# LayerNorm statistics inside a recurrent block: transposes on TensorE against partial sums sent through DRAM

## The chip, the cores and the metric

The kernel runs on one core of one Trainium2 chip. The metric is the device time of one execution in microseconds (us), lower is better. TensorE (PE) multiplies matrices and transposes through an identity matrix, VectorE (DVE), ScalarE (ACT) and GpSimd (POOL) work elementwise, and the SyncE queue (SP) issues nearly all transfers. The engines run their own instruction streams in order and wait for each other by semaphores.

## What is computed

```python
# attention-like block: a recurrence over 32 chunks of 16 positions, for each (batch, head)
def step(W, kv):
    kc, vc = kv
    z = einsum('bhsd,bhde->bhse', kc, W)
    grad = einsum('bhsd,bhse->bhde', kc, (z - vc) * inv_n)
    return (W - LR * grad, z)
out = zs ...                                   # (B, S, 512)
mu = mean(out, axis=-1); var = var(out, axis=-1)
out = (out - mu) * rsqrt(var + 1e-5) * ln_gamma + ln_beta
x = layernorm(x + out @ Wo.T)                  # then a mixture of 8 experts, top 2, and a shared expert
```

The change concerns `mu` and `var` of the recurrence's output: one mean and one variance for each of 2048 tokens, over 512 features.

## The kernel before, in words

The 2048 tokens are ordered so that one step of the recurrence gives 64 tokens and two steps give one **tile** of 128 tokens. There are 16 tiles, 0 to 15. The program is written out slot by slot: each of the 32 steps is two slots, the even one with `scan_z` (z by 64 small matmuls, L548) and `scan_r` (the residual, DVE L559, then four masks on ACT, L562), the odd one with `scan_g` (64 small matmuls, L573, then the new W copied out of PSUM by ACT, L580). The order of every engine's work is that in which `slot` calls the helpers; no planner is involved.

After the scan's own instructions, each slot adds work of three kinds:

- the pipeline of the tiles, by the list `STAGES`: an entry (d, pe, fn) runs fn(i) in slot 4i + d, entries that are not for PE first. For tile i, `out_rows` (POOL, L602 and L604) writes z into `zst` in slot 4i+3; `zt` (DVE, L613) transposes it by blocks of 32x32 into `zT` in slot 4i+4; `t_one` (PE, L618) transposes zT by four 128x128 blocks into bank 6 in slot 4i+5, so that a row of the bank is one token; `hi_z` (ACT, L623) and, in slot 4i+6, `stats_one` (DVE, L628, L589, L590) split zT in two parts for exact products and take the statistics from bank 6; `t_wo_` (PE, L649) multiplies by Wo in slot 4i+7; `stats_two` (DVE L654, L589, L590, POOL L591, L592, L658) scales by the first rstd, adds x and takes the second statistics in slot 4i+8; `norm_two` (ACT, L661) normalizes in slot 4i+9 and stores; `t_three` (PE, L672) transposes the result in slot 4i+10, `router` (L684) follows. So `stats_two(i-1)` stands in the same slot as `zt(i)`, behind it, and `t_three(i-1)` in the slot of `stats_one(i)`.
- filler for PE: the projections of the next quarter (`products`, L444, with the rotary arrangement on DVE L474, L479, L485, L490 and POOL L471, L475), and from slot 47 on the shared expert (`gate_up_steps` L755 with DVE L731 and L255, `down_steps` L779 with DVE L782), whose weights are split on ACT and DVE (L240, L243) and on ACT and POOL (L230, L231).
- loads, all on SP, in program order: `fetch_x`, the stores of `norm_two` and `t_three`, and at slot 48 `load_d(0)` and `load_g(1)`, at slot 64 `load(3)`.

The scan ends with slot 63; slots 64 to 71 drain the tiles. Then come the routing, the rest of the shared expert and the expert stage.

`DV.op`, `PO.op` and the like append an instruction and return a token (semaphore, value); a token given as an argument is waited for. `SP.dma` does the same for a transfer.

Of the kernel before, what the change touches and what calls it, by code (L numbers as in the profile page):

```python
# [6 lines left out]
F32 = mybir.dt.float32  # L7
F32R = mybir.dt.float32r
ALU = mybir.AluOpType
# [5 lines left out]
EPS = 1e-5  # L15
# [80 lines left out]
def program(nc, xT, xtok, wkT, wvT, woT, gam, bet, wg, wgu, wd, wsgu, wsd, cosd, sind, maskd, negid, identd, lowd, constd, upd, out):  # L96
    ctx = ExitStack()
    with ctx:
        def sem(name):
            return ctx.enter_context(nc.semaphore(name))  # L100

        def sb(stack, name, shape, dt=F32):
            return stack.enter_context(nc.sbuf_tensor(name, [128] + shape, dt))

        PE, DV, AC, PO, SP = (Queue(sem(n)) for n in ("s_pe", "s_dve", "s_act", "s_pool", "s_sp"))
        bank = [ctx.enter_context(nc.psum_tensor(f"bank{i}", [128, 512], F32)) for i in range(8)]


        ident = sb(ctx, "ident", [128])
# [3 lines left out]
        mhalf = sb(ctx, "mhalf", [1])  # L113
        mv = sb(ctx, "mv", [4, 2])
        rstd = sb(ctx, "rstd", [4, 2])
# [143 lines left out]
        pa = ExitStack()  # L259
        size = {"late": 0, "first": 0}  # L260

        def part(stack, key, name, shape, dt=F32):
            size[key] += int(np.prod(shape))
            return sb(stack, name, shape, dt)
# [4 lines left out]
        r = part(pa, "late", "r", [2, 2, 512])  # L269
# [3 lines left out]
        zst = part(pa, "late", "zst", [4, 2, 2, 32])  # L273
        zT = part(pa, "late", "zT", [512])
        colsum = part(pa, "late", "colsum", [512])
        oh = part(pa, "late", "oh", [4, 128], F32R)
# [4 lines left out]
        onesr = part(pa, "late", "onesr", [128], F32R)  # L281
        mask = part(pa, "late", "mask", [64])
        wgs = part(pa, "late", "wgs", [4, 8])
        part(pa, "late", "padl", [288])

        vst0 = sb(pa, "vst0", [8, 256])
        vst = (vst0, vst1)
# [48 lines left out]
        d_wkk = [Stream(sem(f"d_wk{k}")) for k in range(4)]  # L336
        d_wvk = [Stream(sem(f"d_wv{k}")) for k in range(4)]
        d_g0 = Stream(sem("d_g0"))
        d_xt = [Stream(sem("d_xt0")), Stream(sem("d_xt1"))]


# [28 lines left out]
        t_mh = PO.op(lambda e: e.memset(mhalf[:], -0.5))  # L370
# [65 lines left out]
        free = {i: () for i in range(8)}  # L436
# [92 lines left out]
        for h in (0, 1):  # L529
            t = PE.op(lambda e, h=h: e.matmul(bank[2 + h][:, 0:256], ident[:], negi[:], start=True, stop=False, skip_group_check=True),  # L530
                      t_ident, t_c2, *free[2 + h])
# [52 lines left out]
        state = {}  # L584
        mvfree = {}

        def norm_stats(src, tok, slot):

            a = DV.op(lambda e: e.bn_stats(st[:, slot, :], src), tok, mvfree.get(slot))  # L589
            b = DV.op(lambda e: e.bn_aggr(mv[:, slot, :], st[:, slot, :]), a)  # L590
            c = PO.op(lambda e: e.tensor_scalar(rstd[:, slot, 0:1], mv[:, slot, 1:2], EPS, None, ALU.add), b)  # L591
            return PO.op(lambda e: e.tensor_tensor(rstd[:, slot, 1:2], rstd[:, slot, 0:1], mhalf[:], ALU.pow), c, t_mh)  # L592

        def out_rows(i):

            par = (i // 4) % 2
            rd = (rdone[2 * i, 0], rdone[2 * i, 1], rdone[2 * i + 1, 0], rdone[2 * i + 1, 1])
            for m in range(2):
                rr = r[:, i % 2, m, :].rearrange("p (a b e) -> p a b e", a=8, b=2)
                zz = za[:, m, :].rearrange("p (a e) -> p a e", a=8)  # L600
                vv = vst[par][:, (2 * i + m) % 8, :].rearrange("p (a e) -> p a e", a=8)
                a = PO.op(lambda e, rr=rr, zz=zz: e.tensor_tensor(zz, rr[:, :, 0, :], rr[:, :, 1, :], ALU.add), *rd)  # L602
                zo = zst[:, :, m, :, :]
                b = PO.op(lambda e, zz=zz, vv=vv, zo=zo: e.tensor_tensor(  # L604
                    zo, zz.rearrange("p (g b) e -> p g b e", g=4), vv.rearrange("p (g b) e -> p g b e", g=4), ALU.add),
                    a, state.get("zT"))
            zst_done[i] = b
            if i % 4 == 3:
                scan_done[i // 4] = (b, gdone[2 * i + 1, 0], gdone[2 * i + 1, 1])
            state["zst"] = b  # L610

        def zt(i):
            state["zT"] = DV.op(lambda e: e.transpose(zT[:], zst[:].rearrange("p a b c d -> p (a b c d)")), state["zst"], state.get("T1"), state.get("oh"))  # L613

        def t_one(i):
            b = 6
            for g in range(4):
                t = PE.op(lambda e, g=g: e.transpose(bank[b][:, g * 128:g * 128 + 128], zT[:, g * 128:g * 128 + 128], ident[:]),  # L618
                          state["zT"], *free[b], inc=(g == 3))
            state["T1"] = t  # L620

        def hi_z(i):
            state["oh"] = AC.op(lambda e: e.activation(oh[:].rearrange("p a b -> p (a b)"), zT[:], ACT.Copy), state["zT"], state.get("WO"))  # L623
# [1 line left out]
        def stats_one(i):  # L625


            state["ol"] = DV.op(lambda e: e.tensor_tensor(ol[:].rearrange("p a b -> p (a b)"), zT[:], oh[:].rearrange("p a b -> p (a b)").bitcast(F32), ALU.subtract),  # L628
                                state["oh"], state["zT"], state.get("WO"))
            state["n1"] = norm_stats(bank[6][:], state["T1"], 0)  # L630
            free[6] = ((DV.sem, DV.count),)

        def fetch_x(i):

# [159 lines left out]
        def down(w, q):  # L794
            for _ in down_steps(w, q):
# [3 lines left out]

        STAGES = [(3, False, fetch_x), (3, False, out_rows), (4, False, zt), (5, True, t_one), (5, False, hi_z), (6, False, residual),
                  (6, False, stats_one), (7, True, t_wo_), (8, False, stats_two),
                  (9, False, norm_two), (10, True, t_three), (11, True, router)]
        later = []
# [13 lines left out]
        def slot(n):  # L819
            q, loc = n // 16, n % 16  # L820
            if n == 48:
                early[:] = [(Q.sem, Q.count) for Q in (PE, DV, AC, PO)]
            todo = [(pe, fn, (n - d) // 4) for d, pe, fn in STAGES
                    if (n - d) % 4 == 0 and 0 <= (n - d) // 4 < NT]
# [102 lines left out]

        LAST = 4 * NT - 4 + STAGES[-1][0]

# [524 lines left out]
```

How the kernel before makes its waits and increments, by code:

```python
    def play(self, eng):  # L69
        for it in self.items:
            if it[0] == "w":
                eng.wait_ge(it[1], it[2])
            elif it[0] == "c":
                _, used, at, fns, other, sem, by = it
                with eng.If_cmp(used[id(self)], at, "IS_GT"):
                    for fn in fns:
                        ins = fn(eng)
                    ins.then_inc(sem, by)
                with eng.Else():
                    other(eng).then_inc(sem, by)
            elif it[0] == "r":
                it[1][id(self)] = eng.to_reg(eng.value_load(it[2], min_val=0, max_val=RT - FULL))
            else:
                ins = it[1](eng)
                if it[2] is not None:
                    ins.then_inc(it[2], it[3])
```

## Time and profile before

| what | value |
|---|---|
| median of three runs | 717.73 us (717.64 to 718.1) |
| profiled execution, its own time | 717.65 us |
| its span, first to last instruction | 715.8 us |
| granted TensorE clock, mean | 0.994 |
| PE busy | 695.0 us (97%) |
| DVE busy | 461.5 us (64%) |
| ACT busy | 341.5 us (48%) |
| POOL busy | 330.0 us (46%) |

The profile is one execution. A view by line groups the instructions of one source line; a timeline puts them in order of start, merging equal neighbours, with the idle time before them and what ended it in brackets. The chain of waits goes back from the last instruction to whatever released each step. Most waits of PE in it are short, since PE has filler in nearly every slot.

### The profile page before, as it was taken

The page shows a single profiled execution, that of the slowest core. Times are in us where ns is not written, and L with a number is a line of the kernel's source. Part 1 is how long each engine was busy: PE and PEld are TensorE (multiplying, and loading weights), DVE is VectorE, ACT ScalarE, POOL GpSimd, SP SyncE. Part 2 cuts the span into 40 slices and gives each one's busy share as a digit, 9 for nine tenths or more (in the row PEclk, how much of TensorE's full clock was granted, in tenths as well). Part 3 has the DMA queues.
Part 4 walks back from the last instruction along what each step waited for, and adds up shares of the span by engine and source line. Part 5 has one row for each costly group of instructions (what it writes and reads, how often), then busy time and mean ns, then how long its engine had stood idle before and what let it go on. Part 6 is the DMA issues. An engine that isn't in the chain of part 4 may idle for free.

```text
span 715.8 us, 17650 instructions
## 1 busy us (share of the span) xinstructions
PE 695.0 (97%) x7388; PEld 583.7 (82%) x7388; DVE 461.5 (64%) x767; ACT 341.5 (48%) x662; POOL 330.0 (46%) x350
## 2 busy tenths in 40 slices
PE   9999999999999999999999999999999899999994
PEld 7767888788877777887888999999988878888883
DVE  4996564585755555378876676666576637767555
ACT  5654444454555442341123677767777542141232
POOL 3667556677555433011003665566574326526232
PEclk9999999999999999999999999999999999999998
DMA  8121131121242414000063798999788966414212
GB/s 291 66 75 47 47 104 47 62 89 34 105 135 76 150 47 147 29 14 1 0 235 103 239 326 291 311 319 327 253 274 259 317 189 196 119 68 118 74 73 89
DMA packets 59584, 102.86 MB, mean 144 GB/s; under 512 B 5296, under 2 KB 20400, under 8 KB 59504
## 3 DMA queue, kind: packets, MB, share of 16 engines
q1 hardware_dynamic: 53824, 83.11, 34.2%
q0 software_dynamic: 5680, 18.62, 8.5%
q8 instruction: 59, 0.97, 0.6%
q14 instruction: 21, 0.17, 0.1%
HBM read 79.95 MB, written 21.76 MB: 142 GB/s over the span
## 4 chain that ended last, share of the span: by engine, by line
PE 79%; DVE 10%; ACT 6%; issue 3%; POOL 0%; POOLq 0%; DVEq 0%; ACTq 0%
PE bank L755 20%; PE bank L444 12%; PE bank L779 10%; PE bank L1203 10%; PE bank L649 7%; PE bank L1250 5%; PE bank L573 4%; PE bank L548 4%; PE bank L1219 2%; PE bank L1176 2%; PE bank L684 2%; DVE GL L255 2%; ACT GH L254 2%; DVE sg L731 1%; ACT ah L254 1%
## 5 line engine op out<-in xcount | busy, mean ns | idle before, releaser
L231 POOL TENSOR_TENSOR xl<-RAW,xh 128x1024 fp32r<-128x1024 f32 x31 | 74.9, 2417 | 113.1 <-ACT xh L230 79.9
L254 ACT ACTIVATE ah<-sg 128x512 fp32r<-128x512 f32 (+1 forms) x64 | 33.6, 525 | 157.9 <-DVE sg L731 157.9
L755 PE MATMUL bank<-XH,GH 128*128 128x512 f32 x256 | 101.8, 398 | 1.5 <-ACT GH L254 0.9
L755 PE MATMUL bank<-XH,GL 128*128 128x512 f32 x256 | 99.9, 390 | 0.0
L755 PE MATMUL bank<-XL,GH 128*128 128x512 f32 x256 | 99.7, 389 | 0.0
L255 DVE TENSOR_TENSOR GL<-RAW,GH 128x1024 fp32r<-128x1024 f32 (+2 forms) x63 | 80.6, 1317 | 9.7 <-ACT GH L254 8.3
L591 POOL TENSOR_SCALAR rstd<-mv 128x1 f32<-128x1 f32 x48 | 15.3, 318 | 135.8 <-DVE mv L590 135.1
L1133 POOL DMA_INDIRECT xg<-x1d,idxu x39 | 49.9, 1281 | 57.0 <-DVE idxu L1114 41.2
L1203 PE MATMUL bank<-RH,GH 128*128 128x256 f32 x256 | 73.8, 288 | 0.8 <-ACT RAW L1260 0.4
L1203 PE MATMUL bank<-RH,GL 128*128 128x256 f32 x256 | 72.4, 283 | 0.0
L1203 PE MATMUL bank<-RL,GH 128*128 128x256 f32 x256 | 72.4, 283 | 0.0
L559 DVE TENSOR_TENSOR r<-bank,vst 128x256 f32<-128x256 f32 x64 | 26.5, 423 | 66.9 <-PE bank L548 66.2
L731 DVE TENSOR_TENSOR sg<-sg,bank 128x512 f32<-128x512 f32 (+1 forms) x64 | 35.0, 548 | 50.6 <-PE bank L755 32.4
L254 ACT ACTIVATE GH<-RAW 128x1024 fp32r<-128x1024 f32 (+2 forms) x67 | 63.5, 998 | 1.4 <-DMA RAW<-in_wgu 1.0
L255 DVE TENSOR_TENSOR al<-sg,ah 128x512 fp32r<-128x512 f32 (+1 forms) x64 | 37.8, 591 | 37.8 <-ACT ah L254 37.8
L562 ACT ACTIVATE r<-r,mask 128x128 f32<-128x128 f32 x128 | 41.0, 391 | 41.5 <-DVE r L559 41.4
L755 PEld LDWEIGHTS bank<-XH,GH 128*128 128x128 f32 x256 | 48.1, 188 | 12.1 <-ACT XH L704 1.3
L755 PEld LDWEIGHTS bank<-XH,GL 128*128 128x128 f32 x256 | 48.0, 188 | 10.4
L755 PEld LDWEIGHTS bank<-XL,GH 128*128 128x128 f32 x256 | 48.1, 188 | 9.4
L444 PE MATMUL bank<-xh,GH 128*128 128x512 f32 x128 | 53.9, 421 | 0.0
L779 PE MATMUL bank<-xh,ah 128*128 128x512 f32 x128 | 50.8, 397 | 1.3 <-DVE x L782 1.0
L1308 POOL DMA_INDIRECT xg<-yd,SI x32 | 34.1, 1064 | 37.7 <-DVE x L1316 23.3
(226 smaller groups left out, 1742.5 us busy)
## 6 DMA issues: line engine op xcount, KB each, us to landing
RAW<-in_wgu SPq DMA_DIRECT2D x21, 1024.0 KB, 8.6
RAW<-in_wd SPq DMA_DIRECT2D x21, 512.0 KB, 6.4
yd<-RAW SPq DMA_DIRECT2D x39, 256.0 KB, 7.5
RAW<-in_wsgu SPq DMA_DIRECT2D x14, 512.0 KB, 4.9
x<-in_xtok SPq DMA_DIRECT2D x16, 256.0 KB, 3.4
x1d<-x SPq DMA_DIRECT2D x16, 256.0 KB, 2.0
RAW<-in_wsd SPq DMA_DIRECT2D x8, 512.0 KB, 4.2
out_x<-x SPq DMA_DIRECT2D x16, 256.0 KB, 2.0
```

The lines of the kernel that those rows point to most:

```text
L231: b = PO.op(lambda e: e.tensor_tensor(DL[:, p, :, :], draw[:, rawp(w), :, :], DH[:, p, :, :].bitcast(F32), ALU.subtract), a, dloaded[w], *f)
L254: a = AC.op(lambda e: e.activation(hi, src, ACT.Copy), *tokens, *free)
L255: b = rest.op(lambda e: e.tensor_tensor(lo, src, hi.bitcast(F32), ALU.subtract), a, *tokens, *free)
L444: t = PE.op(lambda e, k=k, wt=wt, xx=xx, n=n: e.matmul(bank[b][:], wt[:, j, k, hg * 128:hg * 128 + 128], xx[:, k, :], start=(k == 0 and n ...
L562: rtok[h] = AC.op(lambda e, b=b: e.activation(r4[:, :, b, :], r4[:, :, b, :], ACT.Copy, scale=mask[:, 32 * b:32 * b + 1]), s, t_c2)
L649: t = PE.op(lambda e, k=k, aa=aa, ww=ww, n=n: e.matmul(bank[b][:], aa[:, k, :], ww[:, k, :], start=(n == 1), stop=(n == 12)), state["oh"], ...
L731: m = DV.op(lambda e: e.tensor_tensor(sg[:, w, 0:cols], sg[:, w, 0:cols], bank[bu][:, 0:cols], ALU.mult), a, tu)
L755: t = PE.op(lambda e, b=b, k=k, c=c, wt=wt, xx=xx, n=n: e.matmul(bank[b][:], wt[:, p, k, c:c + 128], xx[h][:, k, :], start=(n == 1), stop= ...
L779: t = PE.op(lambda e, b=b, k=k, j=j, aa=aa, ww=ww, n=n: e.matmul(bank[b][:], aa[:, ap, k, j * 128:j * 128 + 128], ww[:, p, k, :], start=(n ...
L1133: PO.items.append(("i", lambda e, h=h: e.indirect_dma_start(xg[:, j % 2, h, :], None, x1d, bass.IndirectOffsetOnAxis(ap=idxu[:, first + h: ...
L1203: t = PE.op(lambda e, b=b, k=k, c=c, wt=wt, xx=xx, n=n: e.matmul(bank[b][:, 0:256], wt[:, pw, k, c:c + 128], xx[:, p, k, :], start=(n == 1 ...
L1250: fns.append(lambda e, b=b, k=k, h=h, aa=aa, ww=ww, n=len(fns): e.matmul(bank[b][:], aa[:, p, k, h * 128:h * 128 + 128], ww[:, pw, k, :], ...
```

## The change

Before, the statistics are read from bank 6, which TensorE fills with four transposes for each tile. After, `t_one` is gone. A new `stat_z` in slot 4i+4, directly behind `zt` and ahead of `stats_two(i-1)`, takes statistics of four pieces of `zst` on DVE (each 128 partitions x 128 elements), which are partial: a token's 512 features lie in four groups of 32 partitions. The four results (24 numbers in each partition) go to a DRAM tensor by one transfer of 12 KB; SP waits until it has landed, and four further transfers bring them back into `sta`, such that a partition holds the four partial statistics of one token. `stats_one` then aggregates these in one instruction. The wait of `zt` for the transposes goes, and `zst` is freed by the last partial statistics. `hi_z`, `stats_one` and all else keep their slots.

```diff
+        stz = part(pa, "late", "stz", [4, 6])
+        sta = part(pa, "late", "sta", [4, 6])
+        d_stz, d_sta = Stream(sem("d_stz")), Stream(sem("d_sta"))
+        zsd = nc.dram_tensor("zsd", (128, 4, 6), F32, kind="Internal").ap()
@@ out_rows
-                    a, state.get("zT"))
+                    a, state.get("zread"))
@@
         def zt(i):
-            state["zT"] = DV.op(lambda e: e.transpose(zT[:], ...), state["zst"], state.get("T1"), state.get("oh"))
-
-        def t_one(i):
-            b = 6
-            for g in range(4):
-                t = PE.op(lambda e, g=g: e.transpose(bank[b][:, g * 128:g * 128 + 128], zT[:, g * 128:g * 128 + 128], ident[:]),
-                          state["zT"], *free[b], inc=(g == 3))
-            state["T1"] = t
+            state["zT"] = DV.op(lambda e: e.transpose(zT[:], ...), state["zst"], state.get("oh"))
+
+        def stat_z(i):
+            for m in range(4):
+                t = DV.op(lambda e, m=m: e.bn_stats(stz[:, m, :], zst[:, :, m // 2, m % 2, :]), state["zst"], state.get("stz"))
+            state["zread"] = t
+            w = SP.dma(zsd, stz[:], d_stz, t, state.get("sta"))
+            state["stz"] = w
+            view = zsd.rearrange("(g r) m s -> m r g s", g=4)
+            for m in range(4):
+                state["sta"] = SP.dma(sta[32 * m:32 * m + 32, :, :], view[m], d_sta, w, state.get("n1a"))
@@ stats_one
-            state["n1"] = norm_stats(bank[6][:], state["T1"], 0)
-            free[6] = ((DV.sem, DV.count),)
+            b = DV.op(lambda e: e.bn_aggr(mv[:, 0, :], sta[:]), state["sta"])
+            state["n1a"] = b
+            c = PO.op(lambda e: e.tensor_scalar(rstd[:, 0, 0:1], mv[:, 0, 1:2], EPS, None, ALU.add), b)
+            state["n1"] = PO.op(lambda e: e.tensor_tensor(rstd[:, 0, 1:2], rstd[:, 0, 0:1], mhalf[:], ALU.pow), c, t_mh)
@@
-        STAGES = [(3, False, fetch_x), (3, False, out_rows), (4, False, zt), (5, True, t_one), (5, False, hi_z), (6, False, residual),
+        STAGES = [(3, False, fetch_x), (3, False, out_rows), (4, False, zt), (4, False, stat_z), (5, False, hi_z), (6, False, residual),
```

## Rows read from the trace of the kernel before

**Rows 1.** The page, part 4: the chain that ended last, shares by engine.
```profile
PE 79%; DVE 10%; ACT 6%; issue 3%; POOL 0%; POOLq 0%; DVEq 0%; ACTq 0%
```

**Rows 2.** View of source line L618: duration ns min/median/max, first and last start.
```profile
L618 PE MATMUL bank<-ident,zT x64: 272/273/329, 47.5 to 278.2; 128*128 128x128 f32 x64
```

**Rows 3.** Timeline of tile 6: start us, us, engine, line, count, [idle before <- releaser].
```profile
134.07 0.87 DVE L559 TENSOR_TENSOR r<-bank,vst 128x256 f32<-128x256 f32 x2 [3.32 <-PE bank L548]
...
134.86 0.70 DVE L613 STREAM_TRANSPOSE zT<-zst 128x512 f32<-128x512 f32 x1
...
138.21 0.27 POOL L658 TENSOR_SCALAR mv<-mv,rstd 128x1 f32<-128x1 f32 x1
138.35 0.66 PE L618 MATMUL bank<-ident,zT 128*128 128x128 f32 x4
...
138.77 0.48 PE L444 MATMUL bank<-xh,GH 128*128 128x512 f32 x1
...
139.29 0.81 ACT L661 ACTIVATE x<-x,mv,rstd 128x512 f32<-128x512 f32 x1
...
141.36 0.66 PE L672 MATMUL bank<-ident,x 128*128 128x128 f32 x4
...
142.67 0.69 DVE L589 BATCH_NORM_STATS2 st<-bank 128x6 f32<-128x512 f32 x1
```

**Rows 4.** Lines of DVE by form: count, busy us, mean ns of one, idle before.
```profile
L589 DVE BATCH_NORM_STATS2 st<-bank 128x6 f32<-128x512 f32 x16 | 11.0, 689 | 0.0
...
L999 DVE TENSOR_TENSOR c<-c 128x128 f32<-128x128 f32 x1 | 0.3, 285 | 0.0
```

**Rows 5.** Chain of waits, routing stretch: start us, us, piece (small DVE operations in a row).
```profile
326.23 0.21 DVE c L999
...
326.46 0.23 DVE sel L1000
```

**Rows 6.** The page, part 6: DMA issues, KB each, median us from issue to landing.
```profile
x<-in_xtok SPq DMA_DIRECT2D x16, 256.0 KB, 3.4
x1d<-x SPq DMA_DIRECT2D x16, 256.0 KB, 2.0
```

**Rows 7.** Timeline of tile 3.
```profile
94.66 0.81 ACT L661 ACTIVATE x<-x,mv,rstd 128x512 f32<-128x512 f32 x1 [0.87 <-POOL mv L658]
...
95.76 0.66 PE L672 MATMUL bank<-ident,x 128*128 128x128 f32 x4
```

**Rows 8.** Timeline of tile 10.
```profile
194.44 0.71 DVE L613 STREAM_TRANSPOSE zT<-zst 128x512 f32<-128x512 f32 x1
...
198.10 0.81 ACT L661 ACTIVATE x<-x,mv,rstd 128x512 f32<-128x512 f32 x1 [0.66 <-POOL mv L658]
...
200.49 0.69 DVE L589 BATCH_NORM_STATS2 st<-bank 128x6 f32<-128x512 f32 x1
```

**Rows 9.** Timeline of tile 11, with the loads of slots 48 and 50.
```profile
206.45 0.38 SPq L62 DMA_DIRECT2D RAW<-in_wsd  x1
...
209.16 0.70 DVE L613 STREAM_TRANSPOSE zT<-zst 128x512 f32<-128x512 f32 x1
...
218.11 1.23 PE L573 MATMUL bank<-r,RAW 32*32 32x64 f32 x64 [0.41 <-ACT r L562]
...
219.02 1.05 ACT L230 ACTIVATE xh<-RAW 128x1024 fp32r<-128x1024 f32 x1
```

**Rows 10.** Timeline of tile 12, at its first filler behind the weights' split.
```profile
233.53 0.50 PE L755 MATMUL bank<-XH,GH 128*128 128x512 f32 x1 [0.33 <-DVE GL L243]
```

**Rows 11.** Timeline of tile 14, where banks 4 and 5 are evacuated.
```profile
263.27 1.27 DVE L782 TENSOR_TENSOR x<-bank,x 128x512 f32<-128x512 f32 x2
...
263.99 0.50 PE L779 MATMUL bank<-xh,ah 128*128 128x512 f32 x1
```

**Rows 12.** Timeline of tile 15, same place in the drain.
```profile
280.88 0.50 PE L779 MATMUL bank<-xh,ah 128*128 128x512 f32 x1 [0.99 <-DVE x L782]
```

**Rows 13.** Timeline of tile 0, its product with Wo.
```profile
54.89 0.47 PE L649 MATMUL bank<-OH,oh 128*128 128x512 f32 x1 [0.35 <-DVE OL L430]
```

More of the change, by code:

```diff
@@ L283, in program @@
         wgs = part(pa, "late", "wgs", [4, 8])
-        part(pa, "late", "padl", [288])
+        stz = part(pa, "late", "stz", [4, 6])
+        sta = part(pa, "late", "sta", [4, 6])
+        part(pa, "late", "padl", [240])
         vst0 = sb(pa, "vst0", [8, 256])
@@ L612, in zt @@
         def zt(i):
-            state["zT"] = DV.op(lambda e: e.transpose(zT[:], zst[:].rearrange("p a b c d -> p (a b c d)")), state["zst"], state.get("T1"), state.get("oh"))
-        def t_one(i):
-            b = 6
-            for g in range(4):
-                t = PE.op(lambda e, g=g: e.transpose(bank[b][:, g * 128:g * 128 + 128], zT[:, g * 128:g * 128 + 128], ident[:]),
-                          state["zT"], *free[b], inc=(g == 3))
-            state["T1"] = t
+            state["zT"] = DV.op(lambda e: e.transpose(zT[:], zst[:].rearrange("p a b c d -> p (a b c d)")), state["zst"], state.get("oh"))
+        def stat_z(i):
[7 more added lines that the diff above has]
+                state["sta"] = SP.dma(sta[32 * m:32 * m + 32, :, :], view[m], d_sta, w, state.get("n1a"))
         def hi_z(i):
```

## Prediction, made before the changed kernel was run

> **What bounds the kernel now.** I read first the chain that ended last [rows 1]: TensorE carries 79% of it, DVE 10%. Then the source line of the removed transposes [rows 2], to see that all 64 exist and stop with the scan's drain, and then timelines, one for each kind of tile. What the reader is to see in the timeline of tile 6 [rows 3] is an engine order with PE at full work: the transposes start at 138.35, the next projection at 138.77, and nobody waits in between. DVE has long pauses in the same stretch (3.32 us before the residual at 134.07). So PE time that is taken away here is worth its full length, as long as the other engines keep their present distance. The other timelines show where they don't have that distance: places at which PE waits, or all but waits, for something behind `stats_two` on DVE.
>
> **What goes.** Four transposes take PE 0.42 us in tile 6 (138.35 to 138.77) [rows 3]; one alone lasts 273 ns, pipelined [rows 2]. Sixteen tiles: 16 x 0.42 = 6.7 us, the most that the change can give. The bank-6 statistics also go from DVE, 689 ns for each tile [rows 4]; they stand behind `ol` and in front of DVE's pauses, where in most tiles nobody waits for DVE, so I count nothing for them.
>
> **What comes on DVE.** Four partial statistics of 128 elements each. The trace has none of that size. Nearest rows: the statistics of 512 elements last 689 ns, other DVE operations with 128 elements in and out 285 ns [rows 4], and such small operations follow each other in steps of 0.23 us [rows 5]. From below: four quarters of 0.69, thus 0.7 us; from above 4 x 0.285 = 1.14 us. I take 4 x 0.23 = 0.92 us, the row of operations in series. The Trainium skill has a rule against just this ("VectorE: DVE Perf Modes", section on the TRN2 errata): latency of SBUF-sourced operations is paid for each instruction, so one large tile pays it once and many small ones each time. Its table (58 cycles plus the elements, at 0.96 GHz) would make 4 x 0.19 = 0.78 us, its measured formula (elements plus 151 cycles) 4 x 0.29 = 1.16 us; the row of 285 ns agrees with the latter. No term below uses these figures.
>
> What matters is where the 0.92 us is put: directly behind `zt(i)` and in front of `stats_two(i-1)` in the same slot. Behind that runs a chain of short operations: DVE L654, L589, L590, POOL L591, L592, L658, ACT L661, and for that PE waits with L672. It all starts 0.92 us later.
>
> **Tiles with cover.** In tile 6, L658 ends at 138.21 + 0.27 = 138.48, L661 starts at 139.29 and ends at 140.10, L672 starts at 141.36 [rows 3]. After: L658 ends at 139.40, L661 at about 140.3, L672 is wanted at 141.36 - 0.42 = 140.94. Cover left 0.6 us, so the gain is whole: -0.42. By the same reading of their timelines this holds for eight tiles (1, 2, 4, 5, 6, 8, 9, 13): 8 x -0.42 = -3.4 us.
>
> **Tiles without.** In tile 3, L661 already waits 0.87 us for POOL, and ends at 94.66 + 0.81 = 95.47, L672 starts at 95.76 [rows 7]: 0.29 us of cover. After, L661 ends at 96.39 and L672 can't start before about 96.45, where the transposes' removal would have had it at 95.34. Against before: +0.7. Tile 7 has the same picture. Tile 10: L661 waits 0.66 us, starts at 198.10 [rows 8] and would end at 199.83, PE wants it about half a us before: +0.5. Tile 11: PE waits 0.41 us there for the masks on ACT, which stand behind L661 and the shared expert's steps [rows 9]; the gain is eaten: 0.
>
> From tile 12 on DVE also splits weights and evacuates banks 4 and 5, behind `stats_two` in the same slots. Tile 12: PE waits 0.33 us for DVE L243 [rows 10], which stands behind the new operations. The transposes' removal only makes this wait longer, and L243 comes 0.92 later: +0.9. Tile 14: L779 starts at 263.99, when the first of the two evacuations from 263.27 is done (1.27 us for two) [rows 11]: +0.9. Tile 15: L779 already waits 0.99 us for L782 [rows 12]: +0.9. In tile 0 the product with Wo waits 0.35 us for DVE L430 [rows 13]; the removed 0.69 stands against the added 0.92 and a wait for the transfers: +0.3.
>
> **Sum.** -3.4 + 0.7 + 0.7 + 0.5 + 0 + 0.9 + 0.9 + 0.9 + 0.3 = +1.5 us. After the drain the work is the same as before and moves as a whole.
>
> **What comes as transfers and waits.** DVE now waits in `stats_one(i)` for four transfers. From the start of `zT` the chain is: 0.70 transpose + 0.92 partial statistics + 2.0 us write (as the 256 KB store of x1, 2.0 us from issue to landing [rows 6]) + three more issues of 0.38 us on SP [rows 9] = 1.14 + 2.0 for the last read = 6.8 us, about 7.0 with the gaps. Room: in tile 6 from 134.86 to 142.67 are 7.8 us [rows 3], less the 0.42 that is gone: 7.4. In tile 10 from 194.44 to 200.49 are 6.05 us [rows 8]: there DVE waits about 1 us. The shorter tiles are 0, 3, 7, 10 and 14. Queued behind the waiting `bn_aggr` on DVE are the rotary operations L479, L485, L490, in tile 10 the split of x for the shared expert, and then the next residual; before that DVE has a pause of 3.3 us (that at 134.07 [rows 3]), so a wait of 1 us costs nothing, save the share in tile 0. POOL waits for the same result ahead of `out_rows(i+1)` and has more than 1 us as well. Bounds of a landing: 2.0 below (no transfer in this trace lands sooner), 3.4 above, the reads of x [rows 6]. With 3.4 for both the chain is 9.6 us, the wait 2.2 us in tiles like 6 (hidden, under 3.3) and 3.5 us in those like 10, which costs PE 1 to 2 us in each of four or five: up to +8 us.
>
> SP waits twice in each tile: for DVE, then about 2 us for the landed write. Behind it stand the stores of x1, the next `fetch_x` and, in tile 11, `load_d(0)` and `load_g(1)`. The latter were issued from 206.45, ahead of zT(11) at 209.16 [rows 9]; now they come behind its reads, at about 209.16 + 0.7 + 0.9 + 2.0 + 4 x 0.38 = 214.3. ACT wants load_d(0) at 219.02 [rows 9]: 4.7 us for a transfer of 512 KB. That is just enough, and ACT has filler work of PE behind it, so 0; were it 3 us later, the next W would be. The stores and `fetch_x` have a tile's length (15 us) to spare. `load(3)` in slot 64 moves equally, and is needed some tens of us later.
>
> So the forecast is 717.65 + 1.5 = 719.15 for the profiled execution, or by the median (717.73) 719.2 us.
>
> **Rivals.**
> (a) *DVE's extra time is covered everywhere*: the chain through POOL and ACT would have to catch up by the start of L672, and L243 and L782 by that of their matmuls. For it: DVE is 64% busy, and the 0.69 us that it loses comes back two slots later. Against it: five places where PE waits, or has under 0.3 us, in the trace of before. It gives 717.65 - 6.7 = 711.0. If only the three to four tiles on ACT's chain are covered, it gives -8 x 0.42 - 4 x 0.42 + 2.7 + 0.3 = -2.0, thus 715.7. Together 0.28.
> (b) *The round trip through DRAM becomes the bound* (the slower side): five dependent transfers of pieces of 96 and 24 bytes. The point from which it decides is a chain of 7.4 + about 2 us, where DVE's pause and POOL's distance to the next zst end. At 3.4 us a landing it costs up to 8 us (727 with the forecast's own loss), at 4.5 us each 16 x about 2 us = 30 us. For it: no transfer of such small pieces stands alone in the trace of before. Against it: 12 KB is nothing beside 256 KB that land in 2.0. The Trainium skill ("DMA: Bandwidth & Descriptors", table of specifications) speaks for it: below 512 bytes a descriptor makes the engine read, modify and write. It gives no time for this, and no row of before shows one. Chance 0.14.
> (c) *SP's order becomes the bound*: load_d(0) or load_g(1) come too late by the 8 us that they are moved, and ACT stands with W behind it. It decides from a landing of over 5 us plus its cover of 4 us; costs 1 to 3 us, once: 721. Chance 0.05.
> (d) *The transposes were no cost to PE*, since PE would only wait elsewhere: forecast without its gain, +4.9 or 722.5. Chance 0.05.
>
> The forecast has 0.48. A measurement of this kernel can tell about 0.2%, 1.4 us, from no change; the forecast's +1.5 lies on that line, so I split its share: 0.26 slower, 0.18 the same, 0.04 faster. Adding the rivals: slower 0.26 + 0.14 + 0.05 + 0.05 = 0.50, the same 0.18 + 0.04 of (a) = 0.22, faster 0.04 + 0.24 = 0.28. The range leaves out the full gain of (a) and the worst of (b): 713 to 725. The likeliest case's own range, from the bounds of the partial statistics (0.7 to 1.14 us in seven places: -1.5 to +1.5), is 717.7 to 720.7.
>
> **What would show it.** Right: no L618; the four partial statistics in steps near 0.23 us and 0.9 in sum; L661 ends about a microsecond later behind zT than before in every tile; PE waits for L661 at L672 in tiles 3, 7 and 10 and not in 6; longer waits of PE for L243 (tile 12) and L782 (tiles 14, 15); reads landed about 7 us after the start of zT, and DVE idle before `bn_aggr` for 1 us or less. Wrong: steps well under 0.2 us, or L661's chain caught up by POOL's pauses; or landings of 3 us and more with DVE idle over 3 us before `bn_aggr`; or ACT L230 waiting for its weights.

## The result, and the profile after

The changed kernel takes 722.55 us (median of five runs, 720.73 to 724.07); the kernel before, run beside it, 718.1 us (five runs, 717.64 to 719.46). The ratio is 1.0073, with a 95% interval of 1.0054 to 1.0093: slower by 4.4 us, where 1.5 was forecast. The measured time lies in the forecast's range of 713 to 725, but above what it gave as the likeliest case's own range, 717.7 to 720.7. The profiled execution took 723.94 us, with a span of 722.1.

The page of after, head and parts 1 and 4 (the chain that ended last), as [rows 1]:

```profile
span 722.1 us, 17659 instructions
...
PE 692.1 (96%) x7324; PEld 579.7 (80%) x7324; DVE 472.7 (65%) x815; ACT 340.5 (47%) x662; POOL 335.2 (46%) x350
...
PE 70%; DVE 14%; ACT 7%; issue 3%; POOL 3%; DMA 2%; SPq 1%; POOLq 0%; DVEq 0%; ACTq 0%
```

PE has 64 instructions fewer and is still on the chain, but with 70% of it instead of 79%: DVE, POOL and the transfers now stand in between. What PE waits for, of after (us in total, times, longest):

```profile
PE bank L789 <- DVE x L792: 3.7, 2, 2.2
...
PE bank L682 <- ACT x L671: 2.9, 4, 0.9
PE bank L659 <- DVE OL L434: 2.4, 1, 2.4
...
PE bank L765 <- DVE GL L243: 1.1, 2, 0.8
```

and the same view of before, where these were short or absent (L672, which is L682 of after, isn't in it):

```profile
PE bank L779 <- DVE x L782: 1.0, 1, 1.0
...
PE bank L649 <- DVE OL L430: 0.4, 1, 0.4
PE bank L755 <- DVE GL L243: 0.3, 1, 0.3
```

These four together are 10.1 us after and 1.7 before: 8.4 us of new waits against 6.7 us of transposes removed. That makes only +1.7. Most of the rest of the loss is time in which PE works, but at a lower clock; it comes below.

**A covered tile.** Timeline of tile 6 of after, to be laid beside [rows 3]:

```profile
137.56 0.70 DVE L617 STREAM_TRANSPOSE zT<-zst 128x512 f32<-128x512 f32 x1
...
138.18 0.83 DVE L622 BATCH_NORM_STATS2 stz<-zst 128x6 f32<-128x128 f32 x4
...
141.68 0.27 POOL L668 TENSOR_SCALAR mv<-mv,rstd 128x1 f32<-128x1 f32 x1
...
143.66 0.66 PE L682 MATMUL bank<-ident,x 128*128 128x128 f32 x4
...
144.88 0.25 DVE L638 BATCH_NORM_AGGREGATE mv<-sta 128x2 f32<-128x24 f32 x1
```

From the transpose to L668 it is 4.12 us where it was 3.35, so the chain of `stats_two` is later by 0.8, and PE doesn't wait.

**A tile without cover.** Timeline of tile 3 of after, as [rows 7]:

```profile
98.36 0.81 ACT L671 ACTIVATE x<-x,mv,rstd 128x512 f32<-128x512 f32 x1 [1.64 <-POOL mv L668]
...
99.22 0.66 PE L682 MATMUL bank<-ident,x 128*128 128x128 f32 x4 [0.87 <-ACT x L671]
```

ACT's wait went from 0.87 to 1.64 us, and PE, which did not wait, waits 0.87.

**By tile.** From one start of the product with Wo to the next tile's (for tile 0 from the start of zT(0)), after less before, read from the two timelines:

| tiles | forecast, each | measured |
|---|---|---|
| 2, 4, 5, 6, 8, 9, 13 | -0.42 | -0.40, -0.41, -0.40, -0.40, -0.34, -0.42, -0.40 |
| 1 | -0.42 | +1.12 |
| 3, 7 | +0.7 | +0.58, +0.59 |
| 10 | +0.5 | +0.54 |
| 11 | 0 | 0.00 |
| 12, 14 | +0.9 | +0.75, +0.81 |
| 15 | +0.9 | +2.37 |
| 0 | +0.3 | +1.64 |
| sum | +1.5 | +5.6 |

The stretch that holds all of this, from the start of zT(0) to the first gather of the expert stage, is the yardstick below. It takes 332.50 us before (45.80 to 378.30) and 338.14 after (46.36 to 384.50): +5.64. What lies outside it took 380.8 to 384.0 us in the ten profiled executions of this document, part of it by a fall of the clock that only five of them have there (last section). So differences of spans and of medians don't agree with the yardstick to the microsecond, and each of its numbers is that of one execution.

Three places stand out: tiles 0, 1 and 15. The timeline of tile 0 of after, to be laid beside [rows 13]:

```profile
53.79 0.26 DVE L638 BATCH_NORM_AGGREGATE mv<-sta 128x2 f32<-128x24 f32 x1 [1.28 <-DMA sta<-zsd]
...
54.60 2.35 DVE L434 TENSOR_TENSOR OL<-x,OH 128x512 fp32r<-128x512 f32 x2
...
54.99 1.41 POOL L479 TENSOR_TENSOR shuf<-shuf,sinT 128x512 f32<-128x512 f32 x1
...
57.09 0.47 PE L659 MATMUL bank<-OH,oh 128*128 128x512 f32 x1 [2.37 <-DVE OL L434]
...
57.40 0.40 PE L659 MATMUL bank<-OL,oh 128*128 128x512 f32 x1
...
59.19 0.63 PE L659 MATMUL bank<-OL,oh 128*128 128x512 f32 x1
```

The same two instructions of DVE in before, with POOL starting 0.2 us before they end:

```profile
53.45 1.29 DVE L430 TENSOR_TENSOR OL<-x,OH 128x512 fp32r<-128x512 f32 x2
...
54.54 1.34 POOL L475 TENSOR_TENSOR shuf<-shuf,sinT 128x512 f32<-128x512 f32 x1
```

PE stands still for 2.37 us, and then its matmuls last 0.63 instead of 0.40 us. And the drain of tile 15, as [rows 12]:

```profile
284.72 1.28 DVE L792 TENSOR_TENSOR x<-bank,x 128x512 f32<-128x512 f32 x2
285.46 0.50 PE L789 MATMUL bank<-xh,ah 128*128 128x512 f32 x1 [2.25 <-DVE x L792]
```

Behind both pauses the granted clock falls. PE by stretches of 1 us, after (stretch, PE busy (instructions), granted clock, DMA share, GB/s):

```profile
57.00:58.00 1.00, 0.91 (x4) 1.00 0.00 0
58.00:59.00 1.00, 1.00 (x5) 0.65 0.00 0
...
60.00:61.00 1.00, 1.00 (x4) 0.50 0.00 0
61.00:62.00 1.00, 1.00 (x34) 0.64 0.00 0
...
286.00:287.00 1.00, 1.00 (x6) 1.00 1.06 359
287.00:288.00 1.00, 1.00 (x6) 0.50 0.98 296
...
290.00:291.00 1.00, 1.00 (x5) 0.80 1.01 363
```

0.50 is 1.2 GHz, 1.00 is 2.4 GHz. Each time some 3 us pass with PE at the lower level. Whether that is a cause of the loss, how large it is, and which part of the change makes the pauses, the experiments had to tell.

### The profile page after: what moved, and what is told of

Same layout as the page of the kernel before. It is cut to its first block, busy times and chain, and to the rows that moved or that the text cites. A ratio compares the mean times of both kernels' runs of the same rounds, so it can differ in the third digit from the quotient of the medians.

```text
span 722.1 us, 17659 instructions
## 1 busy us (share of the span) xinstructions
PE 692.1 (96%) x7324; PEld 579.7 (80%) x7324; DVE 472.7 (65%) x815; ACT 340.5 (47%) x662; POOL 335.2 (46%) x350
## 4 chain that ended last, share of the span: by engine, by line
PE 70%; DVE 14%; ACT 7%; issue 3%; POOL 3%; DMA 2%; SPq 1%; POOLq 0%; DVEq 0%; ACTq 0%
PE bank L765 20%; PE bank L789 10%; PE bank L1213 9%; PE bank L448 7%; PE bank L659 6%; PE bank L1260 5%; PE bank L577 3%; PE bank L552 3%; PE bank L1229 2%; PE bank L1186 2%; DVE GL L255 2%; PE bank L694 2%; ACT GH L254 2%; DVE sg L741 1%; ACT ah L254 1%
## 5 line engine op out<-in xcount | busy, mean ns | idle before, releaser
L563 DVE TENSOR_TENSOR r<-bank,vst 128x256 f32<-128x256 f32 x64 | 26.4, 422 | 57.5 <-PE bank L552 56.9
L595 POOL TENSOR_SCALAR rstd<-mv 128x1 f32<-128x1 f32 x32 | 8.3, 259 | 116.2 <-DVE mv L594 115.6
L789 PE MATMUL bank<-xh,ah 128*128 128x512 f32 x128 | 50.7, 396 | 3.9 <-DVE x L792 3.7
```

The lines of the kernel that those rows point to most:

```text
L789: t = PE.op(lambda e, b=b, k=k, j=j, aa=aa, ww=ww, n=n: e.matmul(bank[b][:], aa[:, ap, k, j * 128:j * 128 + 128], ww[:, p, k, :], start=(n ...
```

## The experiments

Diffs are against the changed kernel unless said otherwise. Each is followed by what was expected before the run.

**The partial statistics alone** (diff against the kernel before; the transposes stay and give the statistics, the partial ones are taken and not used).

```diff
+        def stat_z(i):
+            for m in range(4):
+                t = DV.op(lambda e, m=m: e.bn_stats(stz[:, m, :], zst[:, :, m // 2, m % 2, :]), state["zst"], state.get("stz"))
+            state["zread"] = t
...
-        STAGES = [..., (4, False, zt), (5, True, t_one), ...
+        STAGES = [..., (4, False, zt), (4, False, stat_z), (5, True, t_one), ...
```

> The kernel before plus the four partial statistics of each tile at their new place, whose results nobody reads; the transposes, the statistics from bank 6 and all else as before, no transfers. Theory A (the place of 0.83 us of DVE work ahead of stats_two costs what was lost): the covered tiles 1, 2, 4, 5, 6, 8, 9, 13 show no step against before, tiles 3, 7, 10 about +0.6 us each, 11 +0.2 to +0.4, 12 and 14 and 15 about +0.8 each, tile 0 +0.8 to +1: together about +5, thus 722 to 724 us. Theory B (the round trip through DRAM costs it): no more than +1, 718 to 719.

Measured: 723.84 us (721.11 to 724.74) against 717.75 (715.3 to 719.32), ratio 1.0084 (1.0054 to 1.0114); between the two marks +5.43 us. By tile: 0 in the covered ones, save +0.12 in 2 and 6, +0.89 and +0.87 in 3 and 7, +1.12 in 10, 0 in 11, +0.74, +0.81 and +0.78 in 12, 14 and 15. Tile 3:

```profile
97.33 0.66 PE L682 MATMUL bank<-ident,x 128*128 128x128 f32 x4 [0.53 <-ACT x L671]
```

So four instructions of 0.83 us in sum cost the kernel 5 us, nearly all of it in tiles that the forecast had named as lacking cover. Tile 0 stands at 0.00, where I had expected +0.8 to +1: by themselves the statistics cost nothing there.

**The trip alone** (no partial statistics; a constant is sent through DRAM and aggregated, so the kernel leaves out the true statistics of the recurrence's output).

```diff
+        t_stz = PO.op(lambda e: e.memset(stz[:], 1.0))
@@ stat_z
-            for m in range(4):
-                t = DV.op(lambda e, m=m: e.bn_stats(stz[:, m, :], zst[:, :, m // 2, m % 2, :]), state["zst"], state.get("stz"))
+            t = state["zT"]
             state["zread"] = t
-            w = SP.dma(zsd, stz[:], d_stz, t, state.get("sta"))
+            w = SP.dma(zsd, stz[:], d_stz, t, t_stz, state.get("sta"))
```

> The changed kernel with its transfers and waits, but without the four partial statistics of each tile; a constant is sent through DRAM instead (the statistics of the recurrence's output are left out). Theory A: the transposes' 0.42 us come back in the covered tiles and also in 3, 7, 10 and 11, tiles 12, 14 and 15 stand at 0, tile 0 at 0 to +1: 711.5 to 714 us. Theory B: as the changed kernel or slower than before, over 718.

Measured: 713.32 us (711.88 to 714.61), ratio 0.9940 (0.9923 to 0.9958), between the marks -5.0. Tiles 1 to 10 and 13 are at -0.4 each, 11, 12, 14 and 15 at 0, and tile 0 at -0.59, better than expected: its aggregation doesn't wait for the transfers. In tile 3 ACT's wait is no longer than 0.57, and PE has none:

```profile
92.44 0.81 ACT L671 ACTIVATE x<-x,mv,rstd 128x512 f32<-128x512 f32 x1 [0.57 <-POOL mv L668]
```

This is the gain that removing the transposes is worth, with all five transfers in place: 5.0 of the 6.7 us.

**The statistics without the trip** (no transfers; the aggregation reads the partial statistics where they are, so each partition's result covers a quarter of the features of four tokens instead of one token's).

```diff
-                t = DV.op(lambda e, m=m: e.bn_stats(stz[:, m, :], zst[:, :, m // 2, m % 2, :]), state["zst"], state.get("stz"))
+                t = DV.op(lambda e, m=m: e.bn_stats(stz[:, m, :], zst[:, :, m // 2, m % 2, :]), state["zst"], state.get("n1a"))
...
-            w = SP.dma(zsd, stz[:], d_stz, t, state.get("sta"))
-            state["stz"] = w
-            view = zsd.rearrange("(g r) m s -> m r g s", g=4)
-            for m in range(4):
-                state["sta"] = SP.dma(sta[32 * m:32 * m + 32, :, :], view[m], d_sta, w, state.get("n1a"))
@@ stats_one
-            b = DV.op(lambda e: e.bn_aggr(mv[:, 0, :], sta[:]), state["sta"])
+            b = DV.op(lambda e: e.bn_aggr(mv[:, 0, :], stz[:]), state["zread"])
```

> The changed kernel without its five transfers per tile: the aggregation reads the partial statistics where they lie, so each partition's statistics are those of a quarter of the features (this part of the computation is left out). Theory A: every tile as in the changed kernel, only tile 0 is better by DVE's wait for the transfers (1.3 us) and by what the clock lost behind it (about 1.4 us): 719.5 to 721 us. Theory B: the round trip was the cost, 711 to 714.

Measured: 717.12 us (716.4 to 719.01), ratio 1.0004 (0.9988 to 1.0019), between the marks +1.99. The time is below the 719.5 to 721 that I had expected; outside the marks the profiled execution is 2.5 us shorter than that of before, which had a fall of the clock there that this one hadn't (last section). Tiles 2 to 15 are those of after to 0.1 us, 15 among them with its +2.37; tile 0 is at -0.48 and tile 1 at -0.45. So, with the statistics in place, the trip costs 5.64 - 1.99 = 3.65 us, all at the start: 2.1 us until tile 0's product begins, 1.6 behind it, where the clock now stays up.

Laid side by side, these three runs show that the effects don't add. The statistics alone (+5.43) and the trip alone (-5.00) make +0.4, the change has +5.64. The 5.2 us between them are in tiles 0 (2.2), 1 (1.5) and 15 (1.6). In tile 0 neither part alone costs anything; together they delay the result past the point where DVE wants it. In tile 15 the clock falls behind the pause with the statistics in and the transposes out; with the transposes in, the pause was 1.77 us and the clock stayed.

**Filling PE's two pauses**: idle matmuls of the identity ahead of tile 0's product with Wo and in slot 65; first 20 in each place, then 10 and 9. Everything else is the changed kernel.

```diff
+        def busy(b, count):
+            for n in range(count):
+                t = PE.op(lambda e: e.matmul(bank[b][:, 0:128], ident[:], ident[:], start=True, stop=True), t_ident, *free[b], inc=(n == count - 1))
+            return t
+
+        def keep_on(i):
+            if i == 15:
+                busy(6, 9)
@@ t_wo_
+            if i == 0:
+                busy(7, 10)
@@
-        STAGES = [..., (4, False, stat_z), (5, False, hi_z), ...
+        STAGES = [..., (4, False, stat_z), (5, True, keep_on), (5, False, hi_z), ...
```

> The changed kernel with 20 idle matmuls of PE (128 columns, about 2 us) put into each of its two long pauses: ahead of the product with Wo of tile 0, and in slot 65 ahead of the filler that waits for L792. Theory C (a pause of PE of over 2 us makes the granted clock fall behind it, 1.0 to 0.5 for about 3 us, at a cost of about 1.4 us each time): clock 1.0 in both stretches, and the time falls by 2.5 to 3 us against the changed kernel, to 719.5 to 720 us. Rival (the time is lost in the pauses alone): no change, 722 to 723; if the pauses don't cover the added matmuls, more.

With 20: 724.08 us (722.07 to 724.7), ratio 1.0082 (1.005 to 1.0113), between the marks +6.47. The clock stayed at 1.00 behind both places and tile 1 went to -0.41, but the filling was longer than the pauses. In the drain (the trace has two records for each of the 20 matmuls):

```profile
281.42 4.63 PE L655 MATMUL bank<-ident 128*128 128x128 f32 x40
```

Tile 0's product began 12.76 us behind zT(0) instead of 10.73, so the gain was paid back. This was a badly sized experiment and undecided by its time; hence the second.

> As e5, with 10 idle matmuls ahead of the product with Wo of tile 0 and 9 in slot 65, since 20 took 4.6 us where 2.0 to 2.4 were free. Theory C: the product of tile 0 starts at its time of the changed kernel (57.1 us) or at most 0.2 later, the clock stays at 1.0 behind both pauses, and the two stretches behind them give back 1.5 and 1.6 us: 719 to 721 us. Rival: no gain, since the time behind the pauses is bound by something else: 722 to 724.

With 10 and 9: 719.02 us (717.86 to 719.97) against 716.5 (715.35 to 718.31), ratio 1.0033 (1.0022 to 1.0044), between the marks +2.32, thus 3.3 less than after. PE in the two stretches, first tile 0, then the drain:

```profile
53.54 2.50 PE L655 MATMUL bank<-ident 128*128 128x128 f32 x20
...
55.95 0.47 PE L670 MATMUL bank<-OH,oh 128*128 128x512 f32 x1
```

```profile
57.00:63.00 6.00, 6.00 (x97) 1.00 0.03 5
285.00:292.00 7.00, 7.00 (x36) 1.00 0.59 189
```

Tile 1 is at -0.44 and tile 15 at +0.74, as forecast for them. Work that computes nothing makes this kernel 3 us faster, by keeping the clock: so the clock explains 1.6 us in tile 1 (from +1.12 to -0.44) and 1.6 in tile 15 (from +2.37 to +0.74), 3.2 us of the loss.

**The partial statistics later**, behind `ol` in slot 4i+6 (in DVE's pause), the aggregation at the end of slot 4i+7.

```diff
@@ stats_one
+            stat_z(i)
+
+        def agg(i):
             b = DV.op(lambda e: e.bn_aggr(mv[:, 0, :], sta[:]), state["sta"])
@@
-        STAGES = [..., (4, False, zt), (4, False, stat_z), (5, False, hi_z), ...
+        STAGES = [..., (4, False, zt), (5, False, hi_z), ...
@@ slot
+            if (n - 7) % 4 == 0 and 0 <= (n - 7) // 4 < NT:
+                agg((n - 7) // 4)
```

> The changed kernel, with the four partial statistics moved from slot 4i+4 to slot 4i+6, where the statistics of bank 6 stood (behind ol), and the aggregation to the end of slot 4i+7. Theory A (only the place of the DVE work and of the wait costs): no tile is delayed by stats_two; steps of -0.4 us against before in tiles 1 to 10 and 13, about 0 in 11, 12, 14 and 15, tile 0 between -0.4 and 0, no pause of PE longer than before: 712.5 to 714 us, faster than both kernels. Rival (the transfers, issued two slots later, make the aggregation late for stats_two, or hold zst for the next tile): over 718.

Measured: 717.01 us (714.78 to 719.55), ratio 0.9999 (0.9986 to 1.0012), between the marks -1.37: the loss is gone, but not the gain that I had expected. Tiles 3 and 10 are at -0.4 and 12 at -0.05, as the theory has it. The rest went in three new places. In tile 0 (+0.79) L434 ran beside POOL's L479 and took 2.35 us, and PE waited 1.52:

```profile
53.14 2.35 DVE L434 TENSOR_TENSOR OL<-x,OH 128x512 fp32r<-128x512 f32 x2
...
55.63 0.47 PE L662 MATMUL bank<-OH,oh 128*128 128x512 f32 x1 [1.52 <-DVE OL L434]
```

In the drain the slots are short, and tile 14's result came late for its own `stats_two`, with tile 15's evacuations behind it (+0.14 and +0.69):

```profile
273.47 0.75 DVE L667 SCALAR_TENSOR_TENSOR x<-bank,rstd,x 128x512 f32<-128x512 f32 x1 [0.43 <-POOL rstd L644]
```

The third and largest is behind tile 15's product with Wo, +1.22: its aggregation stands right ahead of its own `stats_two` there, and DVE waits 1.00 us for POOL's rstd (L644) ahead of L667 at 292.84; PE then waits 0.46 us at the transposes L685 and 0.85 at L697.

**The partial statistics behind `stats_two`**, in the same slot.

```diff
-        STAGES = [..., (4, False, zt), (4, False, stat_z), (5, False, hi_z), ..., (8, False, stats_two),
+        STAGES = [..., (4, False, zt), (5, False, hi_z), ..., (8, False, stats_two), (4, False, stat_z),
```

> The changed kernel, with the partial statistics still in slot 4i+4, but behind stats_two of the tile before. Theory A: the chain through L671 is as early as before, so tiles 3, 7 and 10 give -0.4 in place of +0.55; tiles 12, 14 and 15, where weights' splits and evacuations of later in the slot are waited for, keep their +0.8 and the drain its clock loss, tile 0 stays: about 3 us better than the changed kernel, 719 to 720.5. Rival: the transfers, now 1.6 us later, make DVE wait longer and take the gain: 722 to 724.

Measured: 721.52 us (718.98 to 723.13) against 716.5, ratio 1.0073 (1.0049 to 1.0096), between both forecasts. Between the marks it is +3.59; the profiled execution was the shortest of the four. Tiles 7 and 10 gain as expected (-0.05 and -0.41, where after has +0.59 and +0.54), but tile 3 is at +1.85 against before, and 12 at +1.04. Tile 15 is at +0.75: the clock didn't fall there in this execution, which I had expected. The transfers start later and DVE now waits for them ahead of a queue of work:

```profile
87.50 0.26 DVE L638 BATCH_NORM_AGGREGATE mv<-sta 128x2 f32<-128x24 f32 x1 [2.55 <-DMA sta<-zsd]
...
89.58 4.13 DVE L821 TENSOR_TENSOR xl<-xr,xh 128x512 fp32r<-128x512 f32 x4
...
93.63 0.74 DVE L563 TENSOR_TENSOR r<-bank,vst 128x256 f32<-128x256 f32 x2
```

PE's filler waits for the pieces of L821, one after the other, and the residual L563 stands behind L821, and the scan behind the residual:

```profile
91.47 0.50 PE L448 MATMUL bank<-xl,GH 128*128 128x512 f32 x1 [0.18 <-DVE xl L821]
```

This is the mechanism of rival (b), which the change itself shows in tile 0 only: here a wait of 2.55 us meets a full queue on DVE.

**A version with both**: the later place, but tiles 13 and 14 keep the early one (in slot 4i+5, aggregated in 4i+7), and tile 0's low part of Wo (L434, pieces 2 and 3) is moved right behind its partial statistics, ahead of POOL's L479.

```diff
@@ stats_one, with the same agg as in the later place
+            if i not in (13, 14):
+                stat_z(i)
+            if i == 0:
+                wo_low(2)
+                wo_low(3)
+
+        def stat_early(i):
+            if i in (13, 14):
+                stat_z(i)
+
+        def agg_early(i):
+            if i in (13, 14):
+                agg(i)
@@
-        STAGES = [..., (4, False, zt), (4, False, stat_z), (5, False, hi_z), ...
+        STAGES = [..., (4, False, zt), (5, False, stat_early), (7, False, agg_early), (5, False, hi_z), ...
@@
-                if n == 5 + k // 2:
+                if n == 5 and k < 2:
                     wo_low(k)
@@ slot
+            if (n - 7) % 4 == 0 and 0 <= (n - 7) // 4 < NT and (n - 7) // 4 not in (13, 14):
+                agg((n - 7) // 4)
```

> e4 (partial statistics behind ol in slot 4i+6, aggregation at the end of slot 4i+7) with three places changed by what its trace shows: in tiles 13 and 14 the partial statistics stand in DVE's pause of slot 4i+5 and the aggregation ahead of slot 4i+7's filler, and in tile 0 the split of Wo's last two blocks (L434) stands right behind the partial statistics, ahead of the rotary shuffle, so that it doesn't run beside POOL's L479. Theory A (only the place costs): from the first zT to the first gather 329 to 330 us, against 332.5 before and 331.1 in e4; the step of tile 0 falls by about 1, those of tiles 14 and 15 from +0.1 and +0.7 to about 0 or less; 713.5 to 715.5 us where the kernel before has 716.5 to 717.7. Rival: DVE and POOL share more than their places, and the losses appear elsewhere: as e4, 717.

Measured: 714.41 us (713.83 to 714.85) against 717.84 (715.78 to 718.17), ratio 0.9956 (0.9942 to 0.9969): faster than both kernels. The profiled span is 712.2 us. Between the marks it is at -2.53. Tile 0 is at -0.59, tiles 1 to 7, 9 and 13 at -0.4, 8 at -0.22, 11, 12, 14 and 15 at 0. Two places are left. Behind tile 15's product with Wo it loses 1.22 us, as the later place did: tile 15's aggregation still stands right ahead of its `stats_two`, where DVE waits 1.00 us for POOL's rstd. The last transposes come 0.63 us later and the router behind them another 0.6. The other is tile 10 (+0.73), where PE waits for the masks behind the residual:

```profile
192.48 1.23 PE L577 MATMUL bank<-r,RAW 32*32 32x64 f32 x64 [0.73 <-ACT r L566]
```

## Why the prediction was right in sign and small in size

**The reading of cover held.** The partial statistics lie where the forecast put them and last 0.83 us for four (0.92 forecast): 273 ns for one, in steps of (0.83 - 0.27) / 3 = 0.19 us.

```profile
L622 DVE BATCH_NORM_STATS2 stz<-zst x64: 246/273/280, 47.0 to 280.5; 128x6 f32<-128x128 f32 x64
```

The covered tiles gave -0.40 each, and 3, 7, 10, 11, 12 and 14 came within 0.15 us of their terms. That in these tiles the position ahead of `stats_two` is the cause, and not the trip, is shown from both sides: the statistics alone cost 5.4, the trip alone gains 5.0. Of the two figures of the Trainium skill ("VectorE: DVE Perf Modes", section on the TRN2 errata) the 0.78 us by the table was the nearer one here, the 1.16 us by the formula too high.

**Tile 15: the step "+0.9" was mis-sized.** 0.74 of it is the delay (the filled version shows it alone). The other 1.6 us are the clock: with 0.99 us of waiting already there [rows 12], a later L792 together with what is no longer in front of it made one pause of 2.25 us, and behind it PE ran at 1.2 GHz. I had added a delay to a wait and not asked what PE does after so long a pause.

**Tile 0: the step "+0.3" was mis-sized**, by 1.3 us within it and 1.5 in tile 1, where the forecast had -0.42. Its cover [rows 13] was thin, and three things came together: the wait for the transfer (1.28 us, forecast at about that in short tiles), L434 that ran beside POOL's L479 and took 2.35 us instead of 1.29, and the clock behind the pause of 2.37 us. The forecast's +0.3 is 0.92 - 0.69 and leaves 0.07 for "a wait for the transfers", which alone was 1.28; and the 0.92 itself costs this tile nothing without the trip.

These three account for it: 1.3 + 1.5 + 1.5 = 4.3 us more than forecast, the other tiles 0.3 less, thus the +5.6 between the marks. Without them the sum would be +1.3: the forecast's sign rests on the mechanism that it named, not on what it missed. The medians' +4.4 is smaller. Mean clocks of the five runs go with the times: 0.989 in the three of 722.55 to 724.07 us, 0.994 and 0.995 in those of 720.73 and 721.29. That in the latter one fall less happened is likely, but these runs have no trace, so it isn't shown, nor which one: besides the two places above there is a third, outside the marks (last section).

**The transfers: right that they don't bound, wrong in their size.** Of after, the issues of the trip (KB each, median us from issue to landing):

```profile
sta<-zsd SPq DMA_DIRECT2D x64, 3.0 KB, 1.7
...
zsd<-stz SPq DMA_DIRECT2D x16, 12.0 KB, 1.4
```

The forecast held that nothing lands sooner than 2.0 us. That was the smallest row of before, for 256 KB, and no bound. The four reads of a tile keep SP issuing for 1.75 us, as long as one of them takes by the median. For pieces under 512 bytes the Trainium skill ("DMA: Bandwidth & Descriptors", table of specifications) tells of a read, modify and write; pieces of 96 bytes show no price of it here, at 1.4 us. DVE's waits for the result, of after:

```profile
DVE mv L638 <- DMA sta<-zsd: 5.9, 5, 2.0
```

Five in all: 1.28 in tile 0, 0.81, 1.15 and 0.67 in tiles 3, 7 and 10, and 2.02 in tile 13, where the forecast had tile 14. Only the first costs time: without the transfers tiles 3, 7, 10 and 13 are as in after. SP's order, rival (c), did nothing: the load forecast for 214.3 was issued at 216.60 in a kernel that was 2.6 us later by then, and tile 11 is unchanged.

```profile
216.60 0.40 SPq L62 DMA_DIRECT2D RAW<-in_wsd  x1
```

Rival (a) is excluded by the waits at L682 and L789; (d) by the tiles at -0.40 and by the trip alone; (b) has its mechanism in tile 0 (3.65 us for the trip, with the clock, and only together with the statistics), and beyond that it shows only where the statistics were moved behind `stats_two`.

What stays open: why tile 13's transfer took so long (it lies behind a load of 512 KB in time, which is no proof), and what the 0.73 us in tile 10 and the 1.22 in the drain of the best version would come to with the aggregation elsewhere, which no run tried.

## What to carry to other kernels

Price an added instruction by what is queued behind it on its engine and by the cover of that chain in each stage, not by the engine's busy share: 0.83 us on an engine that is 64% busy cost 5 us in six tiles of sixteen and next to nothing in the rest; in the best version, mostly in pauses of DVE, it is 2.5 us slower than the trip alone, where the change is 10.6 us slower. Test two parts of a change together as well as apart: here 5.2 us arose only where both met. Where a wait of PE grows, look at the length of the whole pause, since the clock behind it can cost as much again. A result that travels through DRAM fits best where its wait falls into a pause of the waiting engine with nothing urgent behind it, and that place may differ for the first and the last tiles.

## What the runs showed of the hardware

**The clock behind a pause.** Pauses of PE of 2.37 and 2.25 us (after) were followed by some 3 us at 1.2 GHz, in which a 128x512 matmul comes every 0.43 us instead of 0.23; it cost 1.6 us each time. But the length of the pause doesn't decide alone. These are the ends of the drain's pause in three kernels: the first fell to 0.50, the second and the third stayed at 1.00.

```profile
281.64 0.50 PE L784 MATMUL bank<-xh,ah 128*128 128x512 f32 x1 [2.25 <-DVE x L787]
```

```profile
283.71 0.50 PE L789 MATMUL bank<-xh,ah 128*128 128x512 f32 x1 [2.20 <-DVE x L792]
```

```profile
286.88 0.51 PE L789 MATMUL bank<-xh,ah 128*128 128x512 f32 x1 [1.77 <-DVE x L792]
```

They are, in this order, the statistics without the trip, those behind `stats_two`, and those alone. The clock behind the first two:

```profile
284.00:286.00 2.00, 2.00 (x6) 0.50 0.11 33
```

```profile
284.00:290.00 6.00, 6.00 (x30) 1.00 0.66 199
```

In the latter kernel a shorter pause, 1.96 us in tile 0, did let it fall (mean 0.74 from 57 to 63 us). A third place shows the same, in the expert stage and thus outside the marks. There PE pauses 2.22 us before its matmul at 570.36 in the kernel before, and the clock is at 0.50 from 571 to 573 us; after has such a fall from 578 to 580. The statistics without the trip have the same pause, 2.24 us, and no fall. Of the ten profiled executions five have it (before, after, the 20 idle matmuls, the 10 and 9, the later place); outside the marks they took 382.8 to 384.0 us, the others 380.8 to 382.6. The runs don't say what tells these cases apart, so a difference of 1.5 us between two single executions can be one such fall and nothing of the edit.

**DVE beside POOL.** Two `tensor_tensor` of 128x512 with both inputs in SBUF take 1.29 us on DVE in before, where POOL's own starts 0.20 us before they end, and 2.35 us where it runs beside them. In the best version they take 1.60 us: they start at 52.92, while this `tensor_tensor` of POOL runs for another 0.45 us.

```profile
51.63 1.74 POOL L666 TENSOR_TENSOR x<-x,bias 128x512 f32<-128x512 f32 x1
```

The Trainium skill ("SBUF — State Buffer", section "SBUF: two separate sides") has DVE and GpSimd share one pair of ports; for an instruction of DVE with two inputs in SBUF, against one of GpSimd that reads SBUF, whoever starts first holds it for the whole instruction. The trace agrees: the 1.06 us added are most of the 1.41 us of POOL's instruction, and the 0.31 added in the best version most of the 0.45 us that they overlap.
